# AdaLN transformer block on Trainium2: a pair's four score tiles issued in two groups, with another pair's value product between them

## The chip, the cores and the metric

One core of one Trainium2 chip runs the whole program. The metric is device time in microseconds (us) from start to end of one execution. Its engines are TensorE (PE, with its weight loads shown apart as PEld), VectorE (DVE), ScalarE (ACT), GpSimd (POOL) and the DMA queues, of which SyncE (SP) issues most. Each engine runs its own list of instructions in the order written, and waits on semaphores for the others.

## The reference, cut to what matters

x has shape (8, 512, 128). The attention half, whose inner loop the change reorders, is:

```python
h = _layernorm(x) * (1 + ca) + sa
qkv = einsum('bse,ef->bsf', h, W_qkv)                 # 16 heads of 64
q, k = rotary_embedding(q), rotary_embedding(k)
scores = einsum('bqhd,bkhd->bhqk', q, k) * scale
scores = where(tril(ones((512, 512))), scores, -1e9)  # causal
weights = softmax(scores)
out = einsum('bhqk,bkhd->bqhd', weights, v)
x = x + ga * einsum('bsf,fe->bse', out.reshape(...), W_out)
```

After it comes a top-2 mixture of 8 experts (up, GELU, down), whose result is normalised, gated and added to x. The change doesn't touch that half.

## The kernel before, in words

The attention works on pairs of heads: 8 batches times 8 pairs make 64 pairs (STEPS), one per slot. all_slots writes each engine's list as a sequence of 68 slots. In a slot three pairs are in flight: q0 gets its projections (pe_qk) and its rotation, q1, one behind, gets scores and softmax, and q2, two behind, its transposes, value product and output product. Pieces of the routing of the mixture are spread over the slots (route_pe, route_act, route_dve and others), some only in some of each eight slots.

The scores of a pair are four tiles of 128 query rows, numbered idx 0 to 3, with 512, 128, 384 and 256 key columns (TILES = (3, 0, 2, 1), since the mask is causal), for two heads each. Tile idx takes PSUM banks 2 and 3 (idx 0 and 2) or 4 and 5 (idx 1 and 3). For each tile:

- pe_scores makes it: six matmuls (high and low parts), once the exponentials of the tile that had the banks are done. For idx 2 these are the first two exponentials of the same pair, for idx 3 the third and fourth.
- dve_mask (L1276) adds the causal mask to its last 128 columns, and dve_max (L1283) takes the negated row maximum. They are two VectorE instructions.
- act_exp (L1171) takes two exponentials, one for each head, numbered unit 0 to 7, each with its sum.
- pe_turn_prob (L1090) transposes the result in 128x128 blocks. The six turns are named by query tile and head: 3a and 3b (4 blocks each; from idx 0), 0 (2 blocks), 2a and 2b (3 blocks each), 1 (4 blocks). They alternate between PSUM banks 6 and 7 (PT and PT + 1).
- a store copies each turn to probt: act_store (L1192) or dve_store (L1298).

The rest of a pair: act_rep (L1215) spreads the reciprocal sums of dve_rden, pe_turn_sum (L1099) transposes them, act_r (L1209) copies them out; pe_values (L1112) makes the value product in bank W0 (0); dve_ot (L1306) scales it; pe_out (L1121) makes the output product in bank W1 (1); dve_acc (L1314) adds it to x_all. The bank W1 is the one that pe_qk writes first in the next slot, and the wait for it is written there:

```python
                if due(n - 2):
                    e.wait_ge(v_acc, n - 2)
```

which is the dve_acc of the slot before. pe_qk then writes W0 after a wait for act_v (L1203), the copy of the V tile that pe_v (L1048) makes in each slot. VectorE's dve_u (L1262) and two dve_t (L1267) read both banks after pe_qk. GpSimd's pool_qk and pool_lo finish q and k for the next slot, act_hi (L1199) between them.

The order within a slot is written by hand in pe_slot, act_slot and dve_slot. Before, TensorE issues: pe_qk, turns 0 and 2a, scores 0, turns 2b and 1, the turned sums, scores 1, values, turn 3a, scores 2, pe_out, turn 3b, pe_v, routing, scores 3. VectorE: mask and maximum of the pair in its last slot for tile 3, dve_u, dve_rden, two dve_t, store 2b, mask and maximum 0 and 1, routing, dve_ot, mask and maximum 2, dve_acc, store 3b. ScalarE: exponentials 5 to 7 of the older pair, stores 0 and 2a, act_rep, store 1, act_r, exponentials 0 to 3, store 3a, two act_hi, act_v, exponential 4.

Of the kernel before, what the change touches and what calls it, by code (L numbers as in the profile page):

```python
# [12 lines left out]
P = 128  # L13
# [5 lines left out]
STEPS = B * HP  # L19
# [52 lines left out]
def due(value):  # L72

    return not isinstance(value, int) or value > 0
# [13 lines left out]
def adaln_kernel(nc, x_in, w_qkv, w_out, gate_w, expert_bias, w_up, w_down, c_t, w_mod,  # L88
                 cos_in, sin_in, ident_in, tri_in, rank_in, const_in, out, xs, ys, parts, gates):
    ctx = ExitStack()  # L90
    with ctx:
# [6 lines left out]
        ps = ctx.enter_context(nc.psum_tensor("ps", [P, 8, 512], F32))  # L98
# [870 lines left out]
        with ExitStack() as ph:  # L969
# [11 lines left out]
            rs = sb(ph, "rs", [P, S])  # L981
# [92 lines left out]
            def pe_turn_prob(e, q, u):  # L1074
                n, at = q.n, TURNS.index(u)
                e.wait_ge(a_exp, NU * n + READ[u][-1] + 1)
                if u == "3a":
                    if due(2 * n):
                        e.wait_ge(v_ev, 2 * n)
                elif u == "3b":  # L1080
                    if due(4 * n):
                        e.wait_ge(a_ev, 4 * n)
                elif u == "2a":
                    e.wait_ge(v_ev, 2 * n + 1)
                else:
                    e.wait_ge(a_ev, 4 * n + {"0": 1, "2b": 2, "1": 3}[u])
                at_block = 0
                for unit in READ[u]:
                    for kk in range(TILES[unit // 2] + 1):
                        mm = e.transpose(ps[:, PT + at % 2, at_block * P:(at_block + 1) * P],  # L1090
                                         prob[:, unit, kk * P:(kk + 1) * P], ident[:])
                        at_block += 1
                mm.then_inc(p_t, 1)

            def pe_turn_sum(e, q):
                e.wait_ge(a_rep, q.n + 1)
                e.wait_ge(v_tk, min(q.n + 3, STEPS))
                for i in range(TB):
                    mm = e.transpose(ps[:, W1, i * P:(i + 1) * P],  # L1099
                                     rrep[:, i, :, :].rearrange("p j f -> p (j f)"), ident[:])  # L1100
                mm.then_inc(p_r, 1)

            def pe_values(e, q):
                n = q.n
                e.wait_ge(a_ev, 4 * n + 4)
                e.wait_ge(v_ev, 2 * n + 2)
                e.wait_ge(a_v, n - q.hp % GP + GP)
                e.wait_ge(v_t, min(n + 3, STEPS))
                v, first = val[q.group], (q.hp % GP) * P
                for kk in range(TB):  # L1110
                    for j in range(2):
                        mm = e.matmul(ps[j * HD:(j + 1) * HD, W0, kk * P:S],  # L1112
                                      v[:, kk, first + j * HD:first + (j + 1) * HD],
                                      probt[q.par][:, j, kk, kk * P:S], start=(kk == 0), stop=(kk == TB - 1))
                mm.then_inc(p_vp, 1)
# [9 lines left out]
            def pe_slot(e, i, c):  # L1125
                (q0, q1, q2), v = pairs(i, c), Tile(8 * i + c)
                if q0.live:
                    pe_qk(e, q0)
                if q2.live:
                    spare_read(e, i, c - 1)  # L1130
                    pe_turn_prob(e, q2, "0")
                    pe_turn_prob(e, q2, "2a")
                if q1.live:
                    pe_scores(e, q1, 0)
                if q2.live:
                    pe_turn_prob(e, q2, "2b")
                    pe_turn_prob(e, q2, "1")
                    pe_turn_sum(e, q2)
                if q1.live:
                    pe_scores(e, q1, 1)  # L1140
                if q2.live:
                    pe_values(e, q2)
                if q1.live:
                    pe_turn_prob(e, q1, "3a")
                    pe_scores(e, q1, 2)
                if q2.live:
                    pe_out(e, q2)
                if q1.live:
                    pe_turn_prob(e, q1, "3b")
                if v.live:  # L1150
                    pe_v(e, v)
                if c in SPARE:
                    if q1.live:
                        e.wait_ge(a_ev, 4 * q1.n + 1)
                    elif q2.live:
                        e.wait_ge(v_ev, 2 * q2.n + 2)
                    route_pe(e, i, c)
                if q1.live:
                    pe_scores(e, q1, 3)

            def act_exp(e, q, unit):
                n, idx, j = q.n, unit // 2, unit % 2
# [23 lines left out]
            def act_store(e, q, u):  # L1186
                n = q.n
                e.wait_ge(p_t, 6 * n + TURNS.index(u) + 1)
                if u == "3a" and due(n - 1):
                    e.wait_ge(p_vp, n - 1)  # L1190
                dst, src = turned(q, u)
                e.copy(dst, src).then_inc(a_ev, 1)  # L1192

# [7 lines left out]
            def act_v(e, v):  # L1201
                e.wait_ge(p_v, v.x + 1)
                e.copy(val[v.group][:, v.t, :], ps[:, W0, :]).then_inc(a_v, 1)  # L1203

            def act_r(e, q):
                e.wait_ge(p_r, q.n + 1)
                if due(q.n):
                    e.wait_ge(v_ot, q.n)
                e.copy(rs[:], ps[:, W1, :]).then_inc(a_r, 1)  # L1209

            def act_rep(e, q):
                e.wait_ge(v_rden, q.n + 1)
# [5 lines left out]
            def act_slot(e, i, c):  # L1218
                (q0, q1, q2), v = pairs(i, c), Tile(8 * i + c)
                if q0.live and q0.n < 2:  # L1220
                    load_turn(e, q0, MOVES[2:])
                if q2.live:
                    act_exp(e, q2, 5)
                    act_exp(e, q2, 6)
                    act_exp(e, q2, 7)
                    act_store(e, q2, "0")
                    act_store(e, q2, "2a")
                    act_rep(e, q2)
                    act_store(e, q2, "1")
                    act_r(e, q2)  # L1230
                route_act_part(e, i, c, 0)
                if part(8 * i + c - 1) is not None:
                    part_high(e, 8 * i + c - 1)
                if q1.live:
                    act_exp(e, q1, 0)
                    act_exp(e, q1, 1)
                    act_exp(e, q1, 2)
                    act_exp(e, q1, 3)
                    act_store(e, q1, "3a")
                route_act_part(e, i, c, 1)  # L1240
                if (i, c) == (0, 2):

                    act_v(e, v)
                if q0.live:
                    act_hi(e, q0, 1)
                    act_hi(e, q0, 0)
                if v.live and (i, c) != (0, 2):
                    act_v(e, v)
                if (i, c) == (0, 1):

                    group_root(e, 1, s_var, s_root)
                if q1.live:
                    act_exp(e, q1, 4)
                route_act(e, i, c)

            def dve_u(e, q):
# [35 lines left out]
            def dve_store(e, q, u):  # L1292
                n = q.n
                e.wait_ge(p_t, 6 * n + TURNS.index(u) + 1)
                if u == "3b" and due(n - 1):
                    e.wait_ge(p_vp, n - 1)
                dst, src = turned(q, u)
                e.tensor_copy(dst, src).then_inc(v_ev, 1)  # L1298
# [18 lines left out]
            def dve_slot(e, i, c):  # L1317
                q0, q1, q2 = pairs(i, c)
                if q2.live:
                    dve_mask(e, q2, 3)  # L1320
                    dve_max(e, q2, 3)
                if q0.live:
                    dve_u(e, q0)
                if q2.live:
                    dve_rden(e, q2)
                if q0.live:
                    dve_t(e, q0, 1)
                    dve_t(e, q0, 0)
                if (i, c) == (0, 2):
                    n_factors(e)  # L1330
                if q2.live:
                    dve_store(e, q2, "2b")
                if q1.live:
                    dve_mask(e, q1, 0)
                    dve_max(e, q1, 0)
                    dve_mask(e, q1, 1)
                    dve_max(e, q1, 1)
                route_dve(e, i, c)
                if (i, c) in ((B, 1), (B, 2)):
                    first_table(e, c - 1)  # L1340
                if q2.live:
                    dve_ot(e, q2)
                if q1.live:
                    dve_mask(e, q1, 2)
                    dve_max(e, q1, 2)
                if q2.live:
                    dve_acc(e, q2)
                if q1.live:
                    dve_store(e, q1, "3b")
                route_dve_last(e, i, c)  # L1350

            def pool_wo(e, q):
# [694 lines left out]
```

## Time and profile before

| | |
|---|---|
| time, 3 runs | 994.35, 997.01, 1002.05 us; median 997.01 |
| profiled execution, span | 996.9 us, 21240 instructions; its own time is the span and what lies around it |
| PE busy | 907.6 us (91%) |
| DVE busy | 830.6 us (83%) |
| ACT busy | 740.4 us (74%) |
| POOL busy | 570.1 us (57%) |
| mean granted TensorE clock | 0.967 |

Busy is the time in which an engine worked on an instruction; matmuls are pipelined and their ends are modelled, so that neighbours overlap in the rows. A timeline row gives start, length, engine, line, operation, operands and shape, the number of equal instructions merged (x), and in brackets the idle time before it with the instruction that ended it. The granted clock is the share of full speed that TensorE had: 1.00 is 2.4 GHz, 0.50 is 1.2 GHz. The attention runs from about 20 to 800 us, with its full slots from 48 us on; the mixture fills the rest.

### The profile page before, as it was taken

The numbers are of one execution on the slowest core, as the hardware profiler recorded it, in microseconds if no ns is written. First come the engines' busy times: TensorE is split into PE (matmuls) and PEld (weight loads), VectorE is DVE, ScalarE is ACT, GpSimd is POOL, SyncE is SP. The second block draws the span as 40 slices with busy tenths as digits, with TensorE's granted clock in tenths as the row PEclk, the third lists the DMA queues.
The fourth block names the chain that finished last, engine by engine and source line by source line (L and its number), as shares of the span: only waits on it lengthen the run. The fifth ranks groups of instructions, "written<-read, shape, count | busy, mean of one in ns | idle before, by whom it ended". The sixth has DMA issues, their size and how long they took to land. (4 is left out here: it accounts for less than half of the span.)

```text
span 996.9 us, 21240 instructions
## 1 busy us (share of the span) xinstructions
PE 907.6 (91%) x6278; PEld 659.0 (66%) x6278; DVE 830.6 (83%) x1816; ACT 740.4 (74%) x2070; POOL 570.1 (57%) x687
## 2 busy tenths in 40 slices
PE   5699999999999999999999999999999778999930
PEld 3466667676676677666766767677667556888820
DVE  6588888788988888888888888888998678899847
ACT  4487788878787887788778877787777654777725
POOL 1445456545666477657755675767466356765532
PEclk9799999999999999999999999999999989999975
DMA  8234443333344434433344434333443347899844
GB/s 250 81 93 105 111 109 95 94 93 104 94 109 113 117 99 124 115 93 94 108 118 107 110 112 118 96 100 111 110 108 96 110 162 274 290 317 321 311 136 131
DMA packets 124575, 135.53 MB, mean 136 GB/s; under 512 B 13837, under 2 KB 108571, under 8 KB 120496
## 3 DMA queue, kind: packets, MB, share of 16 engines
q1 hardware_dynamic: 118768, 122.42, 42.5%
q0 software_dynamic: 4544, 8.93, 2.7%
q10 hardware_dynamic: 1152, 2.85, 0.8%
q8 instruction: 52, 0.85, 0.3%
q14 instruction: 59, 0.48, 0.2%
HBM read 51.53 MB, written 39.49 MB: 91 GB/s over the span
## 5 line engine op out<-in xcount | busy, mean ns | idle before, releaser
L1364 POOL TENSOR_TENSOR four<-four 128x512 f32<-128x512 f32 x128 | 161.1, 1280 | 278.7 <-DVE ot L1306 178.2
L1171 ACT ACTIVATE prob<-ps,nmax 128x512 f32<-128x512 f32 (+3 forms) x512 | 264.4, 531 | 51.6 <-DVE nmax L1283 50.9
L1283 DVE TENSOR_REDUCE nmax<-ps 128x2 f32<-128x1024 f32 (+3 forms) x256 | 211.0, 824 | 8.8
L1090 PE MATMUL ps<-ident,prob 128*128 128x128 f32 x1280 | 192.4, 280 | 9.3 <-ACT probt L1192 4.9
L1090 PEld LDWEIGHTS ps<-ident,prob 128*128 128x128 f32 x1280 | 142.3, 141 | 60.3 <-ACT prob L1171 32.8
L1368 POOL TENSOR_TENSOR qk_lo<-four,qk_hi 128x512 fp32r<-128x512 f32 x128 | 163.4, 1300 | 1.5 <-ACT qk_hi L1199 1.5
L1276 DVE TENSOR_TENSOR ps<-ps,tri 128x256 f32<-128x256 f32 x256 | 109.4, 427 | 53.8 <-PE ps L1069 53.3
L1112 PE MATMUL ps<-probt,val 128*64 128x512 f32 (+3 forms) x1024 | 152.6, 440 | 0.0
L1192 ACT COPY probt<-ps 128x512 f32<-128x512 f32 (+2 forms) x256 | 125.2, 524 | 21.1 <-PE ps L1090 21.1
L1199 ACT CAST qk_hi<-four 128x512 fp32r<-128x512 f32 x128 | 79.4, 622 | 79.0 <-POOL four L1364 78.3
L1112 PEld LDWEIGHTS ps<-probt,val 128*64 128x64 f32 x1024 | 68.0, 137 | 74.0 <-issue 59.9
L1064 PE MATMUL ps<-qk_hi 64*128 64x512 f32 (+3 forms) x256 | 105.6, 412 | 5.2 <-POOL qk_lo L1368 5.2
L1990 POOL DMA_INDIRECT results<-y,to_i x78 | 82.3, 1055 | 47.4 <-DVE y L1821 28.8
L1262 DVE TENSOR_TENSOR four<-ps,turn_s 128x1024 f32<-128x1024 f32 x64 | 78.4, 1225 | 35.4 <-PE ps L1034 30.9
L1171 ACT ACTIVATION_READ_ACCUMULATOR prob<-ps,nmax 128x1 f32 x512 | 106.1, 207 | 0.0
L1065 PE MATMUL ps<-qk_hi 64*128 64x512 f32 (+3 forms) x256 | 105.6, 413 | 0.0
L1911 ACT ACTIVATE hf<-ps 128x256 f32<-128x256 f32 (+1 forms) x120 | 53.9, 449 | 39.5 <-PE ps L1762 39.0
L1064 PEld LDWEIGHTS ps<-qk_hi 64*128 64x128 f32 x256 | 47.2, 185 | 53.9 <-issue 33.6
L1067 PE MATMUL ps<-qk_hi,qk_lo 64*128 64x512 f32 (+3 forms) x256 | 82.1, 321 | 0.0
L1066 PE MATMUL ps<-qk_hi,qk_lo 64*128 64x512 f32 (+3 forms) x256 | 82.0, 320 | 0.0
L1069 PE MATMUL ps<-qk_lo,qk_hi 64*128 64x512 f32 (+3 forms) x256 | 82.0, 320 | 0.0
L1068 PE MATMUL ps<-qk_lo,qk_hi 64*128 64x512 f32 (+3 forms) x256 | 82.0, 320 | 0.0
(276 smaller groups left out, 2241.5 us busy)
## 6 DMA issues: line engine op xcount, KB each, us to landing
four<-four SPq DMA_DIRECT2D x252, 128.0 KB
wt<-parts SPq DMA_DIRECT2D x24, 1024.0 KB, 7.2
slots<-fill SPq DMA_DIRECT2D x64, 288.0 KB, 2.8
parts<-split SPq DMA_DIRECT2D x64, 128.0 KB, 2.3
wq_lo<-parts SPq DMA_DIRECT2D x6, 1024.0 KB, 6.3
hb<-h_hi SPq DMA_DIRECT2D x64, 64.0 KB, 2.3
hb<-h_lo SPq DMA_DIRECT2D x64, 64.0 KB, 2.0
plain<-results SPq DMA_DIRECT2D x8, 512.0 KB, 7.5
```

The costliest lines, as they stand in the source:

```text
L1064: e.matmul(o0, hi[top_, 0, cols], hi[top_, 1, 0:w], start=True, stop=False)
L1065: e.matmul(o1, hi[low_, 0, cols], hi[low_, 1, 0:w], start=True, stop=False)
L1067: e.matmul(o1, lo[low_, 0, cols], hi[low_, 1, 0:w], start=False, stop=False)
L1090: mm = e.transpose(ps[:, PT + at % 2, at_block * P:(at_block + 1) * P], prob[:, unit, kk * P:(kk + 1) * P], ident[:])
L1112: mm = e.matmul(ps[j * HD:(j + 1) * HD, W0, kk * P:S], v[:, kk, first + j * HD:first + (j + 1) * HD], probt[q.par][:, j, kk, kk * P:S], st ...
L1171: e.activation(prob[:, unit, 0:w], ps[:, bank_s(idx) + j, 0:w], ACT.Exp, bias=nmax[:, q.par, idx, j:j + 1], accum_out=den[:, q.par, 2 * i ...
L1192: e.copy(dst, src).then_inc(a_ev, 1)
L1276: e.tensor_tensor(block_, block_, tri[:].unsqueeze(1).to_broadcast([P, 2, P]), op=ALU.add).then_inc(v_tri, 1)
L1283: e.tensor_reduce(nmax[:, q.par, idx, :], ps[:, bank:bank + 2, 0:w], AX.X, ALU.max, negate=True).then_inc(v_max, 1)
L1364: e.tensor_tensor(qk[:, cols], tt[:, cols], ur[:, cols], op=ALU.add).then_inc(g_qk, 1)
L1368: e.tensor_tensor(qk_lo[q.par][:, half, :], qk[:, half * S:(half + 1) * S], qk_hi[q.par][:, half, :], op=ALU.subtract).then_inc(g_lo, 1)
L1990: e.indirect_dma_start(ys, bass.IndirectOffsetOnAxis(to_i[:, j % Y, t:t + 1], 0), y4[:, j % Y, t, :], None, bounds_check=2 * B * S - 1, oo ...
```

## The change

On TensorE the four turns 0, 2a, 2b, 1 and the turned sums now stand in one run behind pe_qk. After them come scores 0 and 1 of the next pair, the values of q2, scores 2 and 3, turns 3a and 3b, then pe_out, pe_v and the routing. The turned sums go to bank PT instead of W1, and wait for the ScalarE store that frees it. ScalarE now stores all of 0, 2a, 2b and 1, and VectorE 3a and 3b. All eight exponentials of a pair are issued in its own slot, 4 and 5 ahead of the first act_hi and 6 and 7 between the two. On VectorE dve_rden comes first; mask and maximum of tiles 2 and 3 follow dve_ot, then the stores 3a and 3b, and dve_acc is last. Each turn's wait names the store that now frees its bank. The amount of arithmetic stays as it was.

```diff
--- before.py
+++ after.py
@@ -1075,15 +1075,17 @@
                 n, at = q.n, TURNS.index(u)
                 e.wait_ge(a_exp, NU * n + READ[u][-1] + 1)
                 if u == "3a":
-                    if due(2 * n):
-                        e.wait_ge(v_ev, 2 * n)
+                    if due(4 * n - 1):
+                        e.wait_ge(a_ev, 4 * n - 1)
+                    if due(n):
+                        e.wait_ge(a_r, n)
                 elif u == "3b":
                     if due(4 * n):
                         e.wait_ge(a_ev, 4 * n)
-                elif u == "2a":
-                    e.wait_ge(v_ev, 2 * n + 1)
+                elif u in ("0", "2a"):
+                    e.wait_ge(v_ev, 2 * n + {"0": 1, "2a": 2}[u])
                 else:
-                    e.wait_ge(a_ev, 4 * n + {"0": 1, "2b": 2, "1": 3}[u])
+                    e.wait_ge(a_ev, 4 * n + {"2b": 1, "1": 2}[u])
                 at_block = 0
                 for unit in READ[u]:
                     for kk in range(TILES[unit // 2] + 1):
@@ -1094,9 +1096,9 @@
 
             def pe_turn_sum(e, q):
                 e.wait_ge(a_rep, q.n + 1)
-                e.wait_ge(v_tk, min(q.n + 3, STEPS))
+                e.wait_ge(a_ev, 4 * q.n + 3)
                 for i in range(TB):
-                    mm = e.transpose(ps[:, W1, i * P:(i + 1) * P],
+                    mm = e.transpose(ps[:, PT, i * P:(i + 1) * P],
                                      rrep[:, i, :, :].rearrange("p j f -> p (j f)"), ident[:])
                 mm.then_inc(p_r, 1)
 
@@ -1106,6 +1108,7 @@
                 e.wait_ge(v_ev, 2 * n + 2)
                 e.wait_ge(a_v, n - q.hp % GP + GP)
                 e.wait_ge(v_t, min(n + 3, STEPS))
+                e.wait_ge(v_tk, min(n + 3, STEPS))
                 v, first = val[q.group], (q.hp % GP) * P
                 for kk in range(TB):
                     for j in range(2):
@@ -1130,33 +1133,29 @@
                     spare_read(e, i, c - 1)
                     pe_turn_prob(e, q2, "0")
                     pe_turn_prob(e, q2, "2a")
-                if q1.live:
-                    pe_scores(e, q1, 0)
-                if q2.live:
                     pe_turn_prob(e, q2, "2b")
                     pe_turn_prob(e, q2, "1")
                     pe_turn_sum(e, q2)
                 if q1.live:
+                    pe_scores(e, q1, 0)
                     pe_scores(e, q1, 1)
                 if q2.live:
                     pe_values(e, q2)
                 if q1.live:
+                    pe_scores(e, q1, 2)
+                    pe_scores(e, q1, 3)
                     pe_turn_prob(e, q1, "3a")
-                    pe_scores(e, q1, 2)
+                    pe_turn_prob(e, q1, "3b")
                 if q2.live:
                     pe_out(e, q2)
-                if q1.live:
-                    pe_turn_prob(e, q1, "3b")
                 if v.live:
                     pe_v(e, v)
                 if c in SPARE:
                     if q1.live:
-                        e.wait_ge(a_ev, 4 * q1.n + 1)
+                        e.wait_ge(v_ev, 2 * q1.n + 1)
                     elif q2.live:
-                        e.wait_ge(v_ev, 2 * q2.n + 2)
+                        e.wait_ge(a_r, q2.n + 1)
                     route_pe(e, i, c)
-                if q1.live:
-                    pe_scores(e, q1, 3)
 
             def act_exp(e, q, unit):
                 n, idx, j = q.n, unit // 2, unit % 2
@@ -1186,8 +1185,6 @@
             def act_store(e, q, u):
                 n = q.n
                 e.wait_ge(p_t, 6 * n + TURNS.index(u) + 1)
-                if u == "3a" and due(n - 1):
-                    e.wait_ge(p_vp, n - 1)
                 dst, src = turned(q, u)
                 e.copy(dst, src).then_inc(a_ev, 1)
 
@@ -1206,7 +1203,7 @@
                 e.wait_ge(p_r, q.n + 1)
                 if due(q.n):
                     e.wait_ge(v_ot, q.n)
-                e.copy(rs[:], ps[:, W1, :]).then_inc(a_r, 1)
+                e.copy(rs[:], ps[:, PT, :]).then_inc(a_r, 1)
 
             def act_rep(e, q):
                 e.wait_ge(v_rden, q.n + 1)
@@ -1220,12 +1217,10 @@
                 if q0.live and q0.n < 2:
                     load_turn(e, q0, MOVES[2:])
                 if q2.live:
-                    act_exp(e, q2, 5)
-                    act_exp(e, q2, 6)
-                    act_exp(e, q2, 7)
+                    act_rep(e, q2)
                     act_store(e, q2, "0")
                     act_store(e, q2, "2a")
-                    act_rep(e, q2)
+                    act_store(e, q2, "2b")
                     act_store(e, q2, "1")
                     act_r(e, q2)
                 route_act_part(e, i, c, 0)
@@ -1236,21 +1231,25 @@
                     act_exp(e, q1, 1)
                     act_exp(e, q1, 2)
                     act_exp(e, q1, 3)
-                    act_store(e, q1, "3a")
                 route_act_part(e, i, c, 1)
                 if (i, c) == (0, 2):
 
                     act_v(e, v)
+                if q1.live:
+                    act_exp(e, q1, 4)
+                    act_exp(e, q1, 5)
                 if q0.live:
                     act_hi(e, q0, 1)
+                if q1.live:
+                    act_exp(e, q1, 6)
+                    act_exp(e, q1, 7)
+                if q0.live:
                     act_hi(e, q0, 0)
                 if v.live and (i, c) != (0, 2):
                     act_v(e, v)
                 if (i, c) == (0, 1):
 
                     group_root(e, 1, s_var, s_root)
-                if q1.live:
-                    act_exp(e, q1, 4)
                 route_act(e, i, c)
 
             def dve_u(e, q):
@@ -1292,7 +1291,7 @@
             def dve_store(e, q, u):
                 n = q.n
                 e.wait_ge(p_t, 6 * n + TURNS.index(u) + 1)
-                if u == "3b" and due(n - 1):
+                if u == "3a" and due(n - 1):
                     e.wait_ge(p_vp, n - 1)
                 dst, src = turned(q, u)
                 e.tensor_copy(dst, src).then_inc(v_ev, 1)
@@ -1317,36 +1316,30 @@
             def dve_slot(e, i, c):
                 q0, q1, q2 = pairs(i, c)
                 if q2.live:
-                    dve_mask(e, q2, 3)
-                    dve_max(e, q2, 3)
+                    dve_rden(e, q2)
                 if q0.live:
                     dve_u(e, q0)
-                if q2.live:
-                    dve_rden(e, q2)
-                if q0.live:
                     dve_t(e, q0, 1)
                     dve_t(e, q0, 0)
                 if (i, c) == (0, 2):
                     n_factors(e)
-                if q2.live:
-                    dve_store(e, q2, "2b")
                 if q1.live:
-                    dve_mask(e, q1, 0)
-                    dve_max(e, q1, 0)
-                    dve_mask(e, q1, 1)
-                    dve_max(e, q1, 1)
+                    for idx in (0, 1):
+                        dve_mask(e, q1, idx)
+                        dve_max(e, q1, idx)
                 route_dve(e, i, c)
                 if (i, c) in ((B, 1), (B, 2)):
                     first_table(e, c - 1)
                 if q2.live:
                     dve_ot(e, q2)
                 if q1.live:
-                    dve_mask(e, q1, 2)
-                    dve_max(e, q1, 2)
+                    for idx in (2, 3):
+                        dve_mask(e, q1, idx)
+                        dve_max(e, q1, idx)
+                    dve_store(e, q1, "3a")
+                    dve_store(e, q1, "3b")
                 if q2.live:
                     dve_acc(e, q2)
-                if q1.live:
-                    dve_store(e, q1, "3b")
                 route_dve_last(e, i, c)
 
             def pool_wo(e, q):
```

## Rows read from the trace of the kernel before

**Rows 1.** Windows view: busy us of each engine (count), granted clock, DMA share, GB/s

```profile
60.00:770.00 710.00, 703.74 (x5045) 493.54 (x5046) 611.99 (x1155) 569.09 (x1651) 435.75 (x536) 1.00 0.39 105
```

**Rows 2.** Source view of L1262 from 60 to 770 us, one per slot

```profile
L1262 DVE TENSOR_TENSOR four<-ps,turn_s x61: 1211/1225/1227, 61.5 to 766.5; 128x1024 f32<-128x1024 f32 x61
```

**Rows 3.** Timeline of PE, 447 to 459 us, one slot

```profile
447.48 0.50 PE L1027 MATMUL ps<-h_hi,wq_hi 128*128 128x512 f32 x1
...
448.97 0.71 PE L1090 MATMUL ps<-ident,prob 128*128 128x128 f32 x5
449.60 0.49 PE L1064 MATMUL ps<-qk_hi 64*128 64x512 f32 x1
...
450.57 1.01 PE L1090 MATMUL ps<-ident,prob 128*128 128x128 f32 x7
451.42 0.61 PE L1099 MATMUL ps<-ident,rrep 128*128 128x128 f32 x4
451.97 0.32 PE L1064 MATMUL ps<-qk_hi 64*128 64x128 f32 x1
...
452.45 2.38 PE L1112 MATMUL ps<-probt,val 128*64 128x512 f32 x16
...
455.34 0.44 PE L1064 MATMUL ps<-qk_hi 64*128 64x384 f32 x1
...
457.95 0.40 PE L1050 MATMUL ps<-wq_hi,hb 128*128 128x512 f32 x1
```

**Rows 4.** Timeline of DVE, the same slot

```profile
449.17 1.23 DVE L1262 TENSOR_TENSOR four<-ps,turn_s 128x1024 f32<-128x1024 f32 x1 [0.41 <-PE ps L1034]
...
452.04 0.42 DVE L1276 TENSOR_TENSOR ps<-ps,tri 128x256 f32<-128x256 f32 x1
452.49 1.23 DVE L1283 TENSOR_REDUCE nmax<-ps 128x2 f32<-128x1024 f32 x1
...
455.09 0.69 DVE L1306 TENSOR_TENSOR ot<-ps,rs 128x512 f32<-128x512 f32 x1
456.17 0.43 DVE L1276 TENSOR_TENSOR ps<-ps,tri 128x256 f32<-128x256 f32 x1 [0.39 <-PE ps L1069]
456.63 0.96 DVE L1283 TENSOR_REDUCE nmax<-ps 128x2 f32<-128x768 f32 x1
457.51 0.68 DVE L1314 TENSOR_TENSOR x_all<-ps,x_all 128x512 f32<-128x512 f32 x1
458.11 0.68 DVE L1298 COPY probt<-ps 128x512 f32<-128x512 f32 x1
...
459.77 0.69 DVE L1283 TENSOR_REDUCE nmax<-ps 128x2 f32<-128x512 f32 x1
```

**Rows 5.** Timeline of ACT, the same slot

```profile
450.04 0.78 ACT L1192 COPY probt<-ps 128x256 f32<-128x256 f32 x2
...
451.62 0.59 ACT L1192 COPY probt<-ps 128x512 f32<-128x512 f32 x1 [0.29 <-PE ps L1090]
...
453.75 0.69 ACT L1171 ACTIVATE prob<-ps,nmax 128x512 f32<-128x512 f32 x1 [0.86 <-DVE nmax L1283]
...
455.00 0.20 ACT L1171 ACTIVATION_READ_ACCUMULATOR prob<-ps,nmax 128x1 f32 x1
...
458.93 0.58 ACT L1203 COPY val<-ps 128x512 f32<-128x512 f32 x1
459.41 0.59 ACT L1171 ACTIVATE prob<-ps,nmax 128x384 f32<-128x384 f32 x1
...
461.43 0.77 ACT L1192 COPY probt<-ps 128x256 f32<-128x256 f32 x2
```

**Rows 6.** Windows view where PE has gaps, at the end of the attention and behind it

```profile
780.00:790.00 10.00, 8.71 (x70) 6.16 (x70) 9.03 (x27) 6.01 (x18) 2.93 (x5) 1.00 0.08 24
790.00:800.00 10.00, 6.46 (x35) 4.21 (x35) 3.04 (x10) 4.84 (x11) 0.00 (x0) 0.83 0.65 219
...
820.00:830.00 10.00, 7.59 (x35) 5.70 (x35) 9.49 (x34) 6.14 (x11) 7.66 (x8) 1.00 0.80 252
```

## The prediction

> **What bounds the kernel now.** I read the windows first, to see which engine is full in the attention: from 60 to 770 us TensorE is busy for 703.7 of 710 us at the full clock, VectorE for 612 (86%), ScalarE for 569 [rows 1]. So TensorE sets the pace, and VectorE has about 1.6 us of slack in a slot. Then the one VectorE instruction that comes once per slot, for the period: its starts go from 61.5 to 766.5 us in 60 steps, 11.75 us each [rows 2]. Last, the timeline of one slot, engine by engine, for who waits for whom [rows 3 to 5]. The reader is to see there where VectorE idles, in front of L1262 and of the mask of tile 2, both times for TensorE [rows 4]; and that the addition to x_all (457.51) is done by 458.19, a full microsecond before the next slot's first projection matmul needs its bank, while a store, a mask and a maximum (to 460.46) run on behind it, beside the projections [rows 4]. That overlap of VectorE's tail with TensorE's projections is what the change touches.
>
> **The change, walked through one slot.** No arithmetic is removed or added. One store moves from VectorE to ScalarE and one the other way, about 0.1 us each way, which I count at nothing because neither total binds. What counts is order. I take time 0 at the first projection matmul of a slot, and every step from start to start in the rows, so that overlaps are in it.
>
> TensorE's front. Projections take 448.97 - 447.48 = 1.49 us [rows 3]. Before, turns 0 and 2a (0.63), scores 0 (0.97 at 449.60), the seven blocks of 2b and 1 (0.85) and the sums (0.55) follow, and scores 0 begins at 2.12 [rows 3]. The change puts 2b, 1 and the sums ahead of scores 0. Without any wait scores 0 would begin at 1.49 + 0.63 + 0.85 + 0.55 = 3.52. But waits come in: the turns share two banks, each is freed by a ScalarE store, and scores 0, which hid those stores, is gone from between. A block costs 0.12 us and the last ends 0.28 after its start (1.01 - 6 x 0.12) [rows 3]; ScalarE follows 0.04 later (451.58 to 451.62) [rows 3, 5]; stores of 0 and 2a take 0.78 together, so about 0.4 and 0.5 with their overlap [rows 5]; TensorE resumes about 0.13 after one (450.44 to 450.57). So: turn 0 done 1.89, stored 1.93 to 2.33; 2b starts 2.46, done 2.98, stored 3.02 to 3.52; store 2a ends 2.84, turn 1 starts 2.97; the sums need store 2b: 3.65. Scores 0 starts at 3.65 + 0.55 = 4.20. These waits have no row of before; their bounds are 0 (3.52) and 1.0 us, and I take 0.68.
>
> VectorE and ScalarE. L1262 starts at 1.69, and everything up to the first mask took until 4.56 before, with a store that is gone now [rows 4]. The mask now waits for scores 0: 4.20 + 0.97 + 0.04 = 5.21. Maximum 0 starts 0.45 later and lasts 1.23: done 6.89 [rows 4]. Exponential 0 follows by 0.03, and the second is read out 1.45 after that start (453.75 to 455.20): 8.37 [rows 5]. Scores 2, which takes the same banks, starts 0.14 later (455.20 to 455.34): 8.51 [rows 3, 5]. The value product, started behind scores 0 and 1 (0.97 + 0.48: 5.65), is at VectorE 2.64 later, 8.29 [rows 3, 4]; the scaling (0.69) is over before tile 2 comes. So values are hidden, TensorE idles some 0.5 us for the exponentials, and the routing pieces on VectorE lie in the same gap.
>
> VectorE's tail. Mask 2 comes 0.83 after scores 2 (455.34 to 456.17): 9.34. Then maximum 2 (+0.46), mask 3 (+0.88), maximum 3 (+0.46), store 3a (+0.61: 0.69 less the 0.08 by which wide instructions overlap), store 3b (+0.60), addition to x_all (+0.60) which starts at 12.95 and ends 0.68 later: 13.63 [rows 4]. TensorE's next projections need its bank: with 0.14 for the way, 13.77. TensorE itself had finished by about 12.5: from values to V took 452.45 to 458.35, 5.90 us, of which 2.64 is values, so 3.26 behind scores 2's start, and scores 3 adds at most 0.7: 8.51 + 3.96 = 12.47 [rows 3]. It waits 1.3 us for VectorE. This is the new wait; behind it in TensorE's queue are the projections, and behind those the turns and everything else.
>
> Others. ScalarE issues exponentials 4 to 7 (2.02 us in all, 459.41 to 461.43), two casts and the V copy (0.5 to 0.6 each) behind maximum 2: about 10.78 + 3.65 = 14.4, and the second half of the projections, 0.75 after 13.77, waits for that copy: just in time, with no margin [rows 5]. GpSimd still starts behind the scaling, later by 0.7, and has until the next scores 0, which is itself later. The DMAs follow L1262 and are as many as before. The routing on TensorE goes into the idle 1.3 us, so what it costs in some slots before falls away, and I leave that out of the sum.
>
> **The sum.** 13.77 - 11.75 = 2.02 us a slot. From slot 4, the first with all three pairs, to slot 65 there are 61 periods: +123 us. In the last two slots there are no projections to hold up, and the old tail of exponentials 5 to 7 in the last slot is gone; I count zero, between -3 and +3. 996.9 + 123 = 1120. The profiled span (996.9) and the median (997.01) differ by 0.1, so the same holds for the median: 1120 us.
>
> A page against the rows. The Trainium skill says in "VectorE: DVE Perf Modes", section "The DRAIN you can't avoid", that the next VectorE instruction doesn't start before the pipe is empty. The rows don't show that at this chain's joints: the store at 458.11 starts 0.08 before the addition (457.51 + 0.68) ends [rows 4]. By the page the tail's five joints would cost up to 0.4 us more, an estimate, and the result would be 1145; I follow the rows.
>
> **Rivals.** (A) VectorE's tail and the later scores 0 fit under TensorE's work, and the period stays TensorE's own. For it: VectorE is idle 14% of the time. Against: the slack isn't where the tail is. It decides if the addition ends before 12.3, that is if my walk is 1.3 us too long, and even then TensorE idles for the exponentials; only 2 us less returns 11.75. Below that there is little to win: TensorE is 99% busy [rows 1], so with every gap closed the period is 11.65 and 6 us are saved. 988 to 1000. This is also the case in which the change does nothing that shows. (B) The front costs no waits: scores 0 at 3.52, period 13.09, +82: 1079. For it: the stores are short; against: the waits are in the code, and each turn must be out of its bank. (C) TensorE's clock falls. The engine will be busy about 11.3 of 13.8 us (82%) with a gap of over 1 us in each slot. Rows: at 87% and at 76% busy the clock stayed at 1.00, at 65% it was 0.83, part of the time at the lower level [rows 6]. Chain steps on TensorE are about 5.4 us a slot (3.6 front without waits, 1.0 and 0.8 scores), which double at the lower level. In one slot of ten that is +33, in one of four +82: 1153 to 1202. The Trainium skill ("TensorE: Matmul & The Clock Gate", "What's actually happening") says that the throttled state is the default and that activity releases it, which speaks against this change; rows 6 agree in kind.
>
> **Chances.** Forecast 0.80, B 0.08, C 0.08, A 0.04. The unknown hand-overs, if each of some six is 0.1 longer, give 14.3 and 1152; half the front's waits give 1099. The range 1085 to 1153 holds the forecast with these ends, and misses A, C and much of B. A measurement of this kernel can't tell less than 1% from no change; only A lies there or below: faster 0.02, same 0.03, slower 0.95.
>
> **What would show it.** L1262's period at 13.5 to 14.1 us over the whole attention; TensorE's busy share in 60 to 770 at 80 to 86%; a new wait of L1027 for L1314 of about 1 us, some 60 times; scores 2 (L1064) waiting 0.5 us for L1171; the second turn waiting for L1192; VectorE idle about 1 us ahead of the first mask for L1069. If L1027 waits for nothing, the loop that I closed through the addition isn't the bound and the sum is wrong. If it waits but the period is 13.1, the front is mis-sized; if the granted clock is under 1.00 between 60 and 770, it is C.

## The result: 12.3% slower, with the profile after

| | before | after |
|---|---|---|
| median | 999.53 us (4 runs) | 1123.51 us (4 runs) |
| ratio, 95% interval | | 1.123 (1.1189 to 1.1271) |
| profiled span | 996.9 us | 1120.6 us |

The forecast was 1120 us, from a median of 997.01 before. The page of the kernel after gives the shares; matmul count and arithmetic are the same, but TensorE's share falls from 91% to 82%:

```profile
span 1120.6 us, 21176 instructions
PE 919.0 (82%) x6278; PEld 659.0 (59%) x6278; DVE 839.0 (75%) x1816; ACT 747.7 (67%) x2070; POOL 572.9 (51%) x687
```

The windows view of the same stretch as [rows 1] shows every engine less busy, and the clock still at 1.00. 612 us of work where there were 704 means that fewer slots fit in:

```profile
60.00:770.00 710.00, 611.98 (x4319) 420.78 (x4317) 530.88 (x984) 496.75 (x1421) 371.86 (x454) 1.00 0.34 90
```

The source view of the once-per-slot instruction, which answers to [rows 2], gives the period: (763.2 - 64.3) / 51 = 13.70 us, against 11.75.

```profile
L1261 DVE TENSOR_TENSOR four<-ps,turn_s x52: 1224/1225/1226, 64.3 to 763.2; 128x1024 f32<-128x1024 f32 x52
```

61 periods x 1.95 = 119 us; the spans differ by 123.7. (The last of these instructions starts at 886.4 us after and at 766.5 before; behind it 3.8 us more pass than before.) Before, single periods varied from 11.3 to 12.8 us with the routing in the slot. After, nearly all lie between 13.69 and 13.73: the routing is hidden, as expected of a loop that doesn't pass through it.

The timeline of TensorE in one slot after, to be held against [rows 3]:

```profile
501.00 0.51 PE L1027 MATMUL ps<-h_hi,wq_hi 128*128 128x512 f32 x1 [0.54 <-DVE x_all L1313]
...
501.83 0.50 PE L1032 MATMUL ps<-h_hi,wq_hi 128*128 128x512 f32 x1
...
502.63 0.71 PE L1092 MATMUL ps<-ident,prob 128*128 128x128 f32 x5
503.57 1.07 PE L1092 MATMUL ps<-ident,prob 128*128 128x128 f32 x7 [0.23 <-ACT probt L1189]
504.75 0.63 PE L1101 MATMUL ps<-ident,rrep 128*128 128x128 f32 x4
505.30 0.50 PE L1064 MATMUL ps<-qk_hi 64*128 64x512 f32 x1
...
509.53 0.44 PE L1064 MATMUL ps<-qk_hi 64*128 64x384 f32 x1 [0.68 <-ACT prob L1170]
...
513.07 0.40 PE L1050 MATMUL ps<-wq_hi,hb 128*128 128x512 f32 x1
514.70 0.51 PE L1027 MATMUL ps<-h_hi,wq_hi 128*128 128x512 f32 x1 [1.23 <-DVE x_all L1313]
```

Read it as a list of gaps. TensorE is done with V at 513.47 and resumes at 514.70, when L1313 (the addition to x_all) is over. It waits 0.68 us ahead of scores 2 for the exponentials, and 0.23 in the turns for a store. VectorE's timeline, for [rows 4]:

```profile
502.83 1.22 DVE L1261 TENSOR_TENSOR four<-ps,turn_s 128x1024 f32<-128x1024 f32 x1 [1.78 <-PE ps L1034]
...
506.31 0.43 DVE L1275 TENSOR_TENSOR ps<-ps,tri 128x256 f32<-128x256 f32 x1 [1.06 <-PE ps L1069]
506.77 1.22 DVE L1282 TENSOR_REDUCE nmax<-ps 128x2 f32<-128x1024 f32 x1
...
510.36 0.43 DVE L1275 TENSOR_TENSOR ps<-ps,tri 128x256 f32<-128x256 f32 x1 [0.24 <-PE ps L1069]
...
512.77 1.28 DVE L1297 COPY probt<-ps 128x512 f32<-128x512 f32 x2
513.96 0.68 DVE L1313 TENSOR_TENSOR x_all<-ps,x_all 128x512 f32<-128x512 f32 x1
```

From 510.36 on VectorE waits for nothing until the addition ends at 514.64, and TensorE needs just that last one. VectorE then does one short reciprocal and idles 1.78 us, until the projections are there: the two engines take turns. The view of waits of TensorE from 60 to 880 us (60 slots) says that this is no single slot:

```profile
PE ps L1027 <- DVE x_all L1313: 47.4, 52, 1.3
PE ps L1064 <- ACT prob L1170: 40.8, 60, 0.7
PE ps L1092 <- ACT probt L1189: 13.5, 60, 0.2
```

### The profile page after: what moved, and what is told of

It is laid out like the page before. It is cut to its first block and busy times, and to the rows that moved or that the text cites. A ratio compares the mean times of both kernels' runs of the same rounds, so it can differ in the third digit from the quotient of the medians.

```text
span 1120.6 us, 21176 instructions
## 1 busy us (share of the span) xinstructions
PE 919.0 (82%) x6278; PEld 659.0 (59%) x6278; DVE 839.0 (75%) x1816; ACT 747.7 (67%) x2070; POOL 572.9 (51%) x687
## 5 line engine op out<-in xcount | busy, mean ns | idle before, releaser
L1092 PE MATMUL ps<-ident,prob 128*128 128x128 f32 x1280 | 185.7, 281 | 17.2 <-ACT probt L1189 15.2
L1189 ACT COPY probt<-ps 128x384 f32<-128x384 f32 (+2 forms) x256 | 119.9, 480 | 57.4 <-PE ps L1092 52.0
L1064 PE MATMUL ps<-qk_hi 64*128 64x512 f32 (+3 forms) x256 | 98.9, 386 | 50.3 <-ACT prob L1170 45.6
L1170 ACT ACTIVATION_READ_ACCUMULATOR prob<-ps,nmax 128x1 f32 x512 | 103.7, 203 | 0.0
L1065 PE MATMUL ps<-qk_hi 64*128 64x512 f32 (+3 forms) x256 | 99.0, 387 | 0.0
L1266 DVE TENSOR_TENSOR four<-ps,turn_c 128x512 f32<-128x512 f32 x128 | 81.8, 681 | 0.0
L1297 DVE COPY probt<-ps 128x512 f32<-128x512 f32 x128 | 81.8, 680 | 0.0
```

The costliest lines, as they stand in the source:

```text
L1064: e.matmul(o0, hi[top_, 0, cols], hi[top_, 1, 0:w], start=True, stop=False)
L1065: e.matmul(o1, hi[low_, 0, cols], hi[low_, 1, 0:w], start=True, stop=False)
L1170: e.activation(prob[:, unit, 0:w], ps[:, bank_s(idx) + j, 0:w], ACT.Exp, bias=nmax[:, q.par, idx, j:j + 1], accum_out=den[:, q.par, 2 * i ...
```

## The experiments

Ratios are against the kernel before, run on the same chip: medians 1002.07 (first four), 1000.57 (5 and 6) and 1000.72 us (7 and 8). Periods are from the source view, 60 to 770 us. In brackets behind a measured time stand its ratio and the ratio's 95% interval. The kernel after has 1.123 (1.1189 to 1.1271) and a period of 13.70.

### 1. The addition ahead of the last two stores

```diff
+                if q2.live:
+                    dve_acc(e, q2)
                 if q1.live:
                     dve_store(e, q1, "3a")
                     dve_store(e, q1, "3b")
-                if q2.live:
-                    dve_acc(e, q2)
```

> The changed kernel with the addition to x_all put ahead of the stores 3a and 3b on VectorE, nothing else. Theory 1 (two loops end together: the addition frees the bank of the first projection half, ScalarE's V copy that of the second, the latter 0.05 us ahead of the matmul in the changed kernel's trace): the first half starts 1.1 us earlier, the second half not at all; period 13.7 us, time 1121 us, 1115 to 1124. Theory 2 (VectorE's tail alone is the bound, the V copy is cover): TensorE starts the projections at 12.6 and the whole slot follows: minus 1.1 us a slot, 1055 us. Theory 3 (the front of the slot, late scores and bank waits, costs all of it and the addition is merely the last to report): 1121 us, but with TensorE then not waiting for the V copy.

Measured: 1124.96 us (1.1208, 1.1161 to 1.1255), period 13.73. Theory 1, with the median 1 us above its range of 1115 to 1124. Theory 3 expected nearly the same time, but no wait for the V copy, and there is one. The timeline (all engines) of a slot with routing shows the first half of the projections (L1027) starting without a wait of its own, and the second (L1032) right behind ScalarE's V copy (L1200). The rows below them, from the timeline of TensorE, are the next slot, which has no routing:

```profile
501.93 0.48 PE L1027 MATMUL ps<-h_hi,wq_hi 128*128 128x512 f32 x1
...
502.25 0.61 ACT L1200 COPY val<-ps 128x512 f32<-128x512 f32 x1
...
502.91 0.19 PEld L1032 LDWEIGHTS ps<-h_hi,wq_hi 128*128 128x128 f32 x1 [0.47 <-ACT val L1200]
```

```profile
514.63 0.50 PE L1027 MATMUL ps<-h_hi,wq_hi 128*128 128x512 f32 x1
...
516.61 0.50 PE L1032 MATMUL ps<-h_hi,wq_hi 128*128 128x512 f32 x1 [1.03 <-ACT val L1200]
```

Someone who had read only the longest wait of the kernel after (L1313) would have expected 66 us here. The wait for the V copy, 25.4 us of TensorE's time in this run (29 slots of 60 to 850 us), stood under it. In most slots with routing another wait took its place: the routing piece waited 0.7 us for store 3a, which the move had pushed back, as in the slot above:

```profile
501.52 0.66 PE L606 MATMUL ps<-ident,rows 128*128 128x128 f32 x4 [0.68 <-DVE probt L1297]
```

So this run already holds the wait that experiment 6 stumbles over.

### 2. The V copy ahead of exponentials 6 and 7

```diff
                     act_hi(e, q0, 1)
+                if v.live and (i, c) != (0, 2):
+                    act_v(e, v)
                 if q1.live:
                     act_exp(e, q1, 6)
                     act_exp(e, q1, 7)
                 if q0.live:
                     act_hi(e, q0, 0)
-                if v.live and (i, c) != (0, 2):
-                    act_v(e, v)
```

> The changed kernel with ScalarE's V copy put ahead of exponentials 6 and 7, nothing else. Theory 1: the second projection half no longer waits 0.1 us behind the V copy, the addition still holds the first: minus 0.1 us a slot, 1114 us, 1108 to 1121. Theory 2: no change, 1121. If the V copy by itself were the bound, minus 1 us a slot, 1060.

Measured: 1113.64 us (1.1112, 1.1062 to 1.1161), period 13.60. Theory 1: minus 0.10 us a slot. The gain is small, but its interval lies below that of the kernel after (1.1189 to 1.1271), and the span agrees (1111.8 against 1120.6). The projections, to the first turn, take 1.49 us again, as in the kernel before, and not 1.63:

```profile
511.29 0.50 PE L1027 MATMUL ps<-h_hi,wq_hi 128*128 128x512 f32 x1 [1.23 <-DVE x_all L1313]
...
512.78 0.71 PE L1092 MATMUL ps<-ident,prob 128*128 128x128 f32 x5
```

### 3. Scores 0 back between turns 2a and 2b

```diff
                     pe_turn_prob(e, q2, "2a")
+                if q1.live:
+                    pe_scores(e, q1, 0)
+                if q2.live:
                     pe_turn_prob(e, q2, "2b")
...
                 if q1.live:
-                    pe_scores(e, q1, 0)
                     pe_scores(e, q1, 1)
```

> The changed kernel with scores 0 put back between turns 2a and 2b on TensorE, nothing else. Theory 1 (the chain runs projections, turns, scores 0, maximum, exponentials, scores 2, VectorE's tail, projections): scores 0 starts at 2.1 us instead of 4.3, but VectorE is ready for its mask at 4.0 only, 1.3 earlier than now, and scores 2 is then set by the value product; in all 0.85 us a slot less, 1069 us, 1055 to 1080. If the front didn't count (tail alone, by sum of VectorE's work), no change: 1121. Theory 3 (the front is all): back to 997 to 1005.

Measured: 1075.9 us (1.0734, 1.0687 to 1.078), period 12.95. Of the 1.95 us a slot, 0.75 are due to the place of scores 0; I had expected 0.85. Theory 3, that the front is all, is out. TensorE's view of waits, 60 to 850 us:

```profile
PE ps L1027 <- DVE x_all L1315: 50.8, 52, 1.5
PE ps L1101 <- ACT probt L1191: 13.6, 61, 0.2
...
PE ps L1064 <- ACT prob L1172: 2.4, 12, 0.2
```

The wait for the addition is as long as ever, while the one for the exponentials (40.8 us in the kernel after) has shrunk to 2.4. The other 1.20 us of the 1.95 are not divided up by this run; the wait for the addition, 0.9 us a slot, is the largest that is left in it.

### 4. The kernel before, with only the addition moved behind tile 3's maximum

```diff
                     dve_mask(e, q2, 3)
                     dve_max(e, q2, 3)
+                q3 = Pair(q2.n - 1)
+                if q3.live:
+                    dve_acc(e, q3)
...
-                if q2.live:
+                if q2.n == STEPS - 1:
                     dve_acc(e, q2)
```

> The kernel before with one thing changed: the addition to x_all is moved on VectorE behind the mask and maximum of tile 3, that is to the head of the next slot, ahead of the projections' reader. Order of scores, turns, stores and exponentials stay as before. Theory 1: the bank of the projections is then freed only after scores 3, its mask and maximum and the addition: 11.8 + 0.46 + 0.61 + 0.68 + 0.14 = 13.7 us a slot against 11.75, 1117 us, 1095 to 1125. Theory 3 (grouping and the front cost the time, not the place of the addition): 997 to 1003.

Measured: 1124.69 us (1.122, 1.1173 to 1.1267), a mean period of (756.9 - 62.9) / 50 = 13.88. One VectorE instruction, moved behind three others, costs as much as the whole change, and TensorE waits for it 107.3 us between 60 and 850 us. VectorE's timeline, the view of waits, and the wait that follows in this slot:

```profile
503.46 0.43 DVE L1276 TENSOR_TENSOR ps<-ps,tri 128x256 f32<-128x256 f32 x1 [0.99 <-PE ps L1069]
503.92 0.69 DVE L1283 TENSOR_REDUCE nmax<-ps 128x2 f32<-128x512 f32 x1
504.53 0.68 DVE L1314 TENSOR_TENSOR x_all<-ps,x_all 128x512 f32<-128x512 f32 x1
```

```profile
PE ps L1027 <- DVE x_all L1314: 107.3, 58, 1.9
```

```profile
505.26 0.50 PE L1027 MATMUL ps<-h_hi,wq_hi 128*128 128x512 f32 x1 [1.85 <-DVE x_all L1314]
```

The size came out right by more than one cause: the slots' periods lie at 13.2 us without routing, 13.4 to 14.0 where routing stands ahead of scores 3, and 14.2 to 15.6 where the clock fell (last section). My 13.7 took a slot with routing for all. The test shows that the place of the addition is enough to cost this much, not that the same amount of it acts in the kernel after.

### 5. Experiments 1 and 2 together

The two diffs above.

> The changed kernel with both moves together: the addition ahead of the stores 3a and 3b, and the V copy ahead of exponentials 6 and 7. Each alone gave 0 and minus 9 us. Theory 1 (two loops of nearly equal length): the first projection half can start at 12.6 instead of 13.7, and the rest follows, but ScalarE now holds exponentials 6 and 7, a cast and the spread of the reciprocals in front of the first store of the turns, which comes 0.4 us later behind its turn: period 13.0 us, 1078 us, 1055 to 1090. Theory 2 (effects simply add): 1112 us.

Measured: 1099.88 us (1.0985, 1.0919 to 1.105), period 13.31. The two moves don't add (minus 24 us together, by the medians, against +1 and -10 alone), so both loops were real, and theory 2 (1112 us) is out. But the time is 22 us above what theory 1 had, and outside its range. In the regular part of the stretch, slots without routing take 12.4 to 12.7 us, better than the 13.0 forecast; those with routing 13.4 to 14.2.

### 6. All three moves

> The changed kernel with all three: addition ahead of the stores, V copy ahead of exponentials 6 and 7, scores 0 between turns 2a and 2b. Theory 1: scores 0 covers ScalarE's late store, TensorE has work until 11.6 and the addition is done then; period 11.75 as before, 1000 us, 990 to 1012, since TensorE is full again. If anything else of the change (stores moved, dve_rden first, scores 2 and 3 together, turned sums in the other bank) costs time, the rest shows here: over 1012. Theory 2 (effects add: minus 9, minus 50): 1062 us.

Measured: 1072.37 us (1.0711, 1.0655 to 1.0767), period 12.91. Both theories missed: theory 1 by 72 us, theory 2 by 10. What came is the case that the expectation named beside theory 1: over 1012, something else of the change costs time. And against experiment 3 alone (1075.9 us, 1.0687 to 1.078), the two other moves together gave nothing that the intervals can tell from zero, though without the third move they had given 24 us. Waits of TensorE, 60 to 830 us:

```profile
PE ps L1064 <- POOL qk_lo L1364: 31.1, 35, 1.2
...
PE ps L1027 <- DVE probt L1299: 5.6, 7, 0.8
PE ps L454 <- DVE probt L1299: 4.8, 6, 0.8
PE ps L356 <- DVE probt L1299: 4.8, 6, 0.8
```

L454 and L356 are routing pieces, which use the turns' bank and wait for store 3a (L1299); moving the addition ahead of the stores pushed these back. And scores 0, now early, waits for GpSimd's low half of q, behind a cast that the change put behind exponentials 6 and 7. Periods alternate from 11.6 to 14.1 us. Where a slot without routing ends early, the next one's scores 0 waits 1.18 us for qk_lo.

### 7. On top of it, store 3a ahead of the addition, 3b behind

```diff
+                if q1.live:
+                    dve_store(e, q1, "3a")
                 if q2.live:
                     dve_acc(e, q2)
                 if q1.live:
-                    dve_store(e, q1, "3a")
                     dve_store(e, q1, "3b")
```

> The version with all three moves came out at 1072 us and not at 1000, its slots alternating between 11.6 and 14.1 us: in the trace, TensorE's routing pieces (five of eight slots) wait for store 3a, which the early addition pushed back, and scores 0 waits for GpSimd's low half of q. Here, on top of it, store 3a goes ahead of the addition and 3b stays behind. Theory 4 (third constraint: routing uses the turns' bank and waits for store 3a): slots with routing lose 0.6 us of wait, the others get 0.6 longer since the addition is later; long and short slots move together, mean 12.6 us, 1048 us, 1035 to 1062. If the long slots came from something else (the routing's own work, DMAs), they stay at 13.4 to 14.1 and the mean rises: 1080 or more.

Measured: 1071.37 us (1.0696, 1.0652 to 1.0741), period 12.89. Theory 4 missed its range: store 3a was waited for, but it didn't set the mean. Its wait all but went (L454, the row of experiment 6: 4.8 us, now 1.2), and the slots did move together: the long ones fell from 13.3-14.1 to 12.8-13.2 us, and the short ones rose by 1.0 us, where 0.6 had been expected, to 12.5-12.9, so that the sum is nil. A long and a short slot in a row last the same in both runs, 13.80 + 11.84 us in experiment 6 and 12.81 + 12.80 here. That points to something without store 3a in it that set the pace of the pair, the wait for qk_lo first of all; experiment 8 tests that. Waits of TensorE, 60 to 830 us:

```profile
PE ps L1064 <- POOL qk_lo L1365: 22.5, 41, 0.6
PE ps L1027 <- DVE x_all L1315: 21.1, 27, 0.9
...
PE ps L454 <- DVE probt L1299: 1.2, 6, 0.2
```

### 8. Both casts ahead of exponentials 6 and 7

```diff
+                if q0.live:
+                    act_hi(e, q0, 0)
                 if q1.live:
                     act_exp(e, q1, 6)
                     act_exp(e, q1, 7)
-                if q0.live:
-                    act_hi(e, q0, 0)
```

> The kernel of the run before with both casts of the high halves ahead of exponentials 6 and 7 on ScalarE, so that GpSimd's low half of q, for which scores 0 waits, comes 0.9 us earlier. Theory 5 (fourth constraint: ScalarE's casts, GpSimd's low half, scores 0): that wait disappears, another 0.2 to 0.4 us a slot less, 1030 us, 1015 to 1045; TensorE then waits only for the addition. If the wait was cover for the addition's loop: no change against the run before.

Measured: 1041.56 us (1.0412, 1.0371 to 1.0454), minus 30 us against experiment 7; period 12.46. Theory 5 holds in its cause: 0.43 us a slot, a little more than the 0.2 to 0.4 expected. That the time lies inside its range of 1015 to 1045 is partly luck, since the range counted on 1048 us for experiment 7, which came out 23 us above. TensorE's weight loads, 60 to 830 us:

```profile
PEld ps L1027 <- DVE x_all L1315: 29.8, 41, 1.3
...
PEld ps L1064 <- POOL qk_lo L1365: 7.9, 36, 1.1
```

The wait for qk_lo was 36.5 us in experiment 7. The one for the addition stays at 29.8 (29.7 in experiment 7). No version beats the kernel before, where TensorE is at work for 99% of the attention. Of the change's 124 us, 41 remain here. No run takes them away, and the turned sums' other bank, the swapped stores, dve_rden first and scores 3 next to scores 2 were never undone one by one; TensorE's largest waits left are 21.3 us for the addition and 13.8 us for the store ahead of the turned sums.

## Why the prediction was right

- **Bound before.** TensorE, 11.75 us a slot. Not tested by itself. It fits that none of the eight versions, whatever waits were taken away, came out below the kernel before.
- **The tail behind the addition.** Forecast: the addition starts at 12.95 after the first projection matmul and TensorE resumes at 13.77. Measured: 513.96 - 501.00 = 12.96 and 13.70. The hand-over was 0.06 us (514.64 to 514.70) and not 0.14. Experiment 4 shows the wait at work in the order of before, experiment 3 with scores 0 back in its old place.
- **The front.** Forecast: scores 0 at 4.20, of which 0.68 for bank waits. Measured 4.30: turns, sums and their waits took 2.67 us (505.30 - 502.63) where I had 2.71, and the projections 1.63 where I had 1.49. The difference in the projections is the V copy, which I had called "just in time, with no margin": it had 0.1 us less than none. Experiment 2 gives these 0.10 us back. **Rival B**, a front without bank waits, is out by these rows: without waits the turns and sums would take the forecast's 2.03 us, and they took 0.64 more. Experiment 3 shows what the whole displacement of scores 0 costs: 0.75 us a slot.
- **The middle.** Exponentials to scores 2: forecast 8.51, measured 8.53, with a wait of 0.68 (forecast "some 0.5"). That the two agree so closely is partly luck: the front was 0.10 us late, and the step from ScalarE's last read-out (508.03 + 1.45 = 509.48) to scores 2 took 0.05 us, where the forecast had 0.14. Mask 2 at 9.36, forecast 9.34.
- **The sum.** 2.02 us forecast, 1.95 measured, 61 times: 123 against 119 us. The spans differ by 4.7 us more than 61 periods of 1.95 explain, 3.8 of them behind the last projections, where I had put zero within 3 us either way. The two misses nearly cancel, by luck. Within the slot the same holds on a small scale: 0.10 us too little in the front, 0.09 and 0.08 too much in the two hand-overs to TensorE.
- **Rival A** (TensorE still the bound): refuted by the wait of L1027. **Rival C** (clock): 1.00 from 60 to 770 us. It did turn up in experiment 4: see the last section.
- **The Trainium skill on the DRAIN** ("VectorE: DVE Perf Modes", section "The DRAIN you can't avoid"): the same section goes on to say that a next instruction which is not held starts earlier, which the prediction left out. In the tail after, the additions and stores still start before their forerunners end (512.77, two copies of 0.68 in 1.28 us; the addition at 513.96 ahead of 514.05). Whether they are held in the page's sense no run shows. The measurement decides for the rows: 1120, not 1145.
- **What I left out** is the depth of the stack. I had named the V copy's margin, but not the routing's wait for store 3a, nor the cast that now stands behind two exponentials. Apart from the V copy's 0.1 us a slot, none of these set the time of this change: the wait that was measured in its trace is the addition's. They decided what the repairs gave, and there I was wrong three times (5, 6, 7).

## What to carry to other kernels

When an order is changed, close the loop: find the last instruction of one engine that the first of another waits for, and walk from it round to itself with start-to-start times. The period is that of the longest loop, however idle each engine is. An instruction that frees a bank belongs as early as its inputs allow, and what nobody is waiting for belongs behind it; experiments 1 and 6 show that the stores which looked like that were waited for by the routing. And before promising what the removal of the largest wait will give, look for the second that ends at the same time: here the addition held the first half of the projections and the V copy the second, only 0.1 us apart in what they cost, and either fix alone gave 0 to 10 us.

## What the runs showed of the hardware

Two kernels with almost the same busy share were granted different clocks; what differs most plainly is how the idle time lay, but no run varies that alone. In the kernel after, TensorE was busy for 612 of 710 us, with gaps of up to 1.3 us, and was granted 1.00 throughout; so it was in experiment 3, with gaps of up to 1.5 us. In experiment 4, about as busy (614 of 710, some of it matmuls made longer by the clock itself), with one gap of 1.85 us in each slot, it was granted 0.97. Windows view of experiment 4, PE alone:

```profile
330.00:335.00 5.00, 4.11 (x35) 1.00 0.39 116
335.00:340.00 5.00, 4.04 (x17) 0.75 0.10 34
340.00:345.00 5.00, 5.00 (x38) 0.91 0.84 219
```

Its timeline shows the same matmul of scores 0 in two neighbouring slots, each some 2 to 3 us behind the end of such a gap (321.96 and 335.96), once at 2.4 GHz and once at 1.2 GHz:

```profile
324.10 0.50 PE L1064 MATMUL ps<-qk_hi 64*128 64x512 f32 x1
...
325.00 0.98 PE L1090 MATMUL ps<-ident,prob 128*128 128x128 f32 x7
...
338.66 0.79 PE L1064 MATMUL ps<-qk_hi 64*128 64x512 f32 x1
...
340.24 1.28 PE L1090 MATMUL ps<-ident,prob 128*128 128x128 f32 x7
```

Windows view of these two stretches, from scores 0 to the turns behind it:

```profile
324.10:325.00 0.90, 0.90 (x8) 1.00 0.23 82
338.66:340.24 1.58, 1.58 (x7) 0.50 0.32 96
```

At the lower level scores 0 took 1.58 instead of 0.90 us, 1.76 times as long, where the prediction's rival C had counted double.

So rival C did come, in a kernel whose order I had not suspected of it, and only in some slots: all 52 starts of the projections between 60 and 770 us come behind a gap of 1.84 to 1.86 us, and the clock fell behind 13 of them. What sets the difference between the slots stays open; I tried nothing to settle it.
